# Expert layers over all tokens replaced by chosen experts on sorted rows, with result transfers placed between row transfers on GpSimd

## What is computed

```python
def reference(x, queries, ln1_w, ln2_w, wqkv, wo, gate_w, w13, w2):
    x = x + linear_attention(layernorm(x), queries)
    return x + ffn(layernorm(x), ...)
# ffn:
    h = rmsnorm(x, ln1_w); q, k, v = split(h @ wqkv.T); q, k = rope(q), rope(k)
    x = x + softmax(causal(q @ k.T * scale)) @ v @ wo.T
    h = rmsnorm(x, ln2_w).reshape(-1, HID)
    rprobs = softmax(h @ gate_w.T)
    topw, topi = top_k(rprobs, 2); topw = topw / sum(topw)
    wfull = zeros((T, E)).at[arange(T)[:, None], topi].set(topw)
    for e in range(8):
        w1, w3 = w13[e, :256], w13[e, 256:]
        out = out + ((silu(h @ w1.T) * (h @ w3.T)) @ w2[e].T) * wfull[:, e:e + 1]
    return x + out
```

## Time and profile before

| | us |
|---|---|
| median of 3 runs (lowest 431.62, highest 436.45) | 433.2 |
| the profiled execution: device time | 435.69 |
| its span in the profile | 434.0 |
| PE busy in the span | 415.7 (96%) |
| DVE busy | 342.6 (79%) |
| ACT busy | 287.8 (66%) |
| POOL busy | 216.6 (50%) |

### The profile page before, as it was taken

One profiled execution on the slowest core, in us unless ns is written; L12 is line 12 of the kernel. 1 busy time (PEld: TensorE's weight loads), 2 busy tenths in 40 slices (PEclk: granted clock), 3 DMA queues, 4 the chain that ended last, 5 costly groups with the idle time before them and its releaser, 6 DMA issues.

```text
span 434.0 us, 8892 instructions
## 1 busy us (share of the span) xinstructions
PE 415.7 (96%) x3032; PEld 255.0 (59%) x3032; DVE 342.6 (79%) x569; ACT 287.8 (66%) x577; POOL 216.6 (50%) x359
## 2 busy tenths in 40 slices
PE   8987997999999999999999999999999999999995
PEld 4743444545455454554545445468788877888883
DVE  6895688779889898998989976546668998787773
ACT  3743653778878688786877869765775565555552
POOL 5100646336147364473744034135883886676673
PEclk9998985599999999999999999899999999999999
DMA  7914202001611010100100000043221223421200
GB/s 219 319 47 137 57 2 56 2 2 40 201 34 28 4 59 0 34 26 4 57 3 5 0 3 3 2 76 74 62 58 37 87 60 66 97 66 57 95 1 24
DMA packets 16983, 23.92 MB, mean 55 GB/s; under 512 B 2622, under 2 KB 7614, under 8 KB 16942
## 3 DMA queue, kind: packets, MB, share of 16 engines
q1 hardware_dynamic: 15982, 22.21, 18.5%
q0 software_dynamic: 960, 1.18, 1.1%
HBM read 18.08 MB, written 5.05 MB: 53 GB/s over the span
## 4 chain that ended last, share of the span: by engine, by line
PE 67%; DVE 16%; issue 9%; ACT 4%; POOL 2%; DMA 1%; POOLq 0%; DVEq 0%; ACTq 0%
PE o_bank L1503 16%; PE tb L1486 11%; PE sp L1443 10%; PE tb L1635 6%; PE sp L1635 6%; DVE mx L1089 5%; PE o_bank L1611 4%; DVE mx L1087 3%; PE sp L1449 2%; PE sp L1463 2%; PE o_bank L1614 2%; ACT pt L893 2%; DVE sw L1287 2%; POOL gl L668 1%; DVE stats L984 1%
## 5 line engine op out<-in xcount | busy, mean ns | idle before, releaser
L893 ACT ACTIVATE pt<-tb 128x512 f32<-128x512 f32 (+2 forms) x310 | 153.4, 564 | 51.6 <-PE tb L1486 46.1
L1089 DVE TENSOR_REDUCE mx<-sp 128x2 f32<-128x1024 f32 (+1 forms) x128 | 143.4, 1155 | 22.5 <-PE sp L1449 13.6
L668 POOL TENSOR_TENSOR gl<-gg,gh 128x512 fp32r<-128x512 f32 x64 | 89.1, 1394 | 46.5 <-ACT gh L944 46.3
L1443 PE MATMUL sp<-k_stk,q_stk 62*128 62x512 f32 (+3 forms) x384 | 83.8, 432 | 4.1 <-DVE mx L1089 1.0
L1486 PE MATMUL tb<-q_stk,k_stk 64*128 64x512 f32 (+3 forms) x372 | 85.4, 413 | 1.6 <-ACT pt L893 1.1
L1503 PE MATMUL o_bank<-pt,v_all 128*32 128x512 f32 (+3 forms) x768 | 82.4, 511 | 0.0
L643 POOL TENSOR_TENSOR tick<-tick 128x1 f32<-128x1 f32 x96 | 18.8, 196 | 120.5 <-ACT pt L893 120.1
L1486 PEld LDWEIGHTS tb<-q_stk,k_stk 64*128 64x128 f32 x372 | 43.1, 193 | 51.0 <-ACT pt L893 40.9
L1287 DVE TENSOR_TENSOR sw<-silu,wbc 128x512 f32<-128x512 f32 x62 | 54.6, 881 | 21.1 <-ACT silu L955 20.8
L955 ACT ACTIVATE silu<-tb 128x512 f32<-128x512 f32 x64 | 38.2, 597 | 38.1 <-PE tb L1635 37.8
L1443 PEld LDWEIGHTS sp<-k_stk,q_stk 62*128 62x128 f32 x384 | 41.7, 198 | 28.1 <-DVE mx L1089 11.4
(11 more groups left out here) (224 smaller groups left out, 577.5 us busy)
## 6 DMA issues: line engine op xcount, KB each, us to landing
wbc<-g_scr SPq DMA_DIRECT2D x31, 256.0 KB, 3.3
w13r<-w_t SPq DMA_DIRECT2D x1, 2048.0 KB, 10.6
q_scr<-q_hi SPq DMA_DIRECT2D x8, 256.0 KB, 3.0
q_stk<-q_scr SPq DMA_DIRECT2D x20, 96.0 KB
x<-x_in SPq DMA_DIRECT2D x4, 256.0 KB, 3.8
q_scr<-q_lo SPq DMA_DIRECT2D x4, 256.0 KB, 3.3
result<-x SPq DMA_DIRECT2D x4, 256.0 KB, 2.5
k_stk<-k_scr SPq DMA_DIRECT2D x10, 96.0 KB
```

Of the source, the lines that this page charges most:

```text
L668: pool.tensor_tensor(gl[m % 4][:, :], gg[m % NGG][:, :], gh[m % 4][:, :].bitcast(F), ALU.subtract).then_inc(d_lo, 1)
L893: act.activation(pt[:, p0:p0 + 2 * len(heads) - 1:2, 0:w], src, ACT.Exp).then_inc(e_done, 1)
L1089: dve.reduce_max(half[:, :, t, i % TC], src[:, :, 0:w], AX.X).then_inc(s_free, 1)
L1443: last = pe.matmul(dst[:, k, w * x:w * (x + 1)], q_stk[n % NQ][rows_[k], i // TC, pair, P * (i % TC):P * (i % TC + 1)], k_stk[n % NQ][rows ...
```

## The change

Each token's row of 128 features is written twice, once for each of its two experts, into a DRAM tensor `xs_d` where the rows stand sorted by expert, each expert's part filled up to a multiple of 128 rows. That gives at most NT = 23 tiles of 128 rows a batch. A 129th column holds the row's place in the result. All multiplications of the third stage are now in plain fp32 (`w13`, `w2` are used as loaded), one tile at a time, with the expert's number in a register of PE; the gates are applied when the results are added to x.

- **Routing.** DVE works out each row's place (`places`, `c_rows`) and each tile's expert (`c_experts`); PE counts with `ranks`.
- **Sending.** POOL writes the rows with indirect DMAs (`send`), 16 of 128 rows a batch. SP fills `xs_d` with zeros ahead of it (`fill`, 12 transfers in periods 3 to 6) and reads the sorted rows back (`load_rows`, 5 transfers).
- **A tile j**: transpose (`turn_rows`), times ln2 on ACT, one matmul with 512 columns (`up`), silu on ACT, product on DVE, two transposes (`turn_products`), a copy on DVE, two matmuls of 128 columns (`down`), a copy on ACT; POOL writes the 128 rows to their places in `z_d` with an indirect DMA (`bring_back`), 23 a batch. At the end SP loads `z_d` (`load_results`) and DVE adds (`add_up`).
- **Batch 0's steps** move from period 7 into periods 4 (attn), 5 (wo, square, norm, htr) and 6 (logits, choice, places), as words of `EXTRA`, and its 16 sends stand between the masks of periods 6 and 7. The fp32r halves of weights and activations and their transfers are gone.
- **Batch 1's steps** stand between batch 0's tiles, as before between steps; its sends follow behind the 11th result of batch 0, one result brought back behind each.

```diff
+EXTRA = {
+    4: {"s7.0.0": "c.a0", "s5.2.1": "c.a1"},
+    5: {"s1.2.0": "c.w0", "s6.1.0": "c.w1", "p2": "x.sq0", "p3": "x.sq1", "p4.0": "x.sq2", "p4.1": "x.sq3",
...
+SENDS = 4
...
 SECOND = {
...
+    "pe": {-1: "o1", 0: "attn0 attn1", 2: "wo0 wo1", 7: "htr0 htr1", 9: "logits", 13: "rank"},
...
+    "dve": {-1: "o1", 2: "sum0", 3: "sum1", 5: "norm0", 6: "norm1", 9: "first", 10: "equal lead", 11: "rest second",
+            12: "sums", 13: "places", 15: "gates"},
 }
-ROOT = 8
...
+NT = (NPAIR + E * (P - 1)) // P
...
+LOADS = ((0, 2), (2, 5), (5, 11), (11, 17), (17, NT))
+OUTS_ROOT, OUTS_FIRST = 4, 11
+ADD_AT = 16, 19
...
+            def load_rows(b):
+                sp.wait_ge(sent[b], 16 * 2 * T)
+                for q, (j0, j1) in enumerate(LOADS):
+                    sp.dma_start(xs[b][:, j0:j1, :], xs_d[b][P * j0:P * j1, :].rearrange("(j p) w -> p j w", p=P)
+                                 ).then_inc(ld_rows[b][q], 16)
...
+            def load_results(b):
+                sp.wait_ge(back[b], 16 * NT)
...
+            def send(b, i):
+
+                k, t = i % 2, i // 2
+                pool.indirect_dma_start(xs_d[b], bass.IndirectOffsetOnAxis(ap=pos[b][:, k, t:t + 1], axis=0),
+                                        h2x[b][k][:, t, :], None, bounds_check=NT * P - 1,
+                                        oob_is_err=False).then_inc(sent[b], 16)
...
+                    elif s == TC and n == 6:
+                        twin()
+                        pool.wait_ge(ld_fill, 16 * B * N_FILL)
+                        pool.wait_ge(c_pos, 1)
+                        for _ in range(SENDS):
+                            send(0, next(sends))
...
+                        if n == NG - 1 or (n == NG - 2 and s >= TC):
+                            for i in itertools.islice(sends, 1):
+                                send(0, i)
...
+            add_residual(0)
+            for j in range(OUTS_FIRST):
+                bring_back(0, j)
+                if j + 1 == OUTS_ROOT:
+                    c_root(1)
+            pool.wait_ge(c_pos, 2)
+            pool.wait_ge(c_h, 4)
+            pool.wait_ge(c_tw, 4)
+            for i in range(2 * T):
+                send(1, i)
+                if OUTS_FIRST + i < NT:
+                    bring_back(0, OUTS_FIRST + i)
+            add_residual(1)
+            for j in range(NT):
+                bring_back(1, j)
...
+            def add_up(b, c):
+
+                dve.wait_ge(ld_z[b][c], 32)
+                dve.wait_ge(d_x, 2 * b + c + 1)
+                for k in range(2):
+                    for t in range(TC * c, TC * (c + 1)):
+                        row = x[:, T * b + t, :]
+                        last = dve.scalar_tensor_tensor(row, z[b][:, k, t, :], gate_w[:, b, k, t:t + 1], row,
+                                                        ALU.mult, ALU.add)
...
+            for b in range(B):
+                pe.wait_ge(c_te, b + 1)
...
+                for j in range(-2, NT + 2):
+                    if j + 2 < NT:
+                        turn_rows(b, j + 2)
+                    if 0 <= j < NT:
+                        up(NT * b + j, of[j])
+                    if j >= 2:
+                        down(NT * b + j - 2, of[j - 2])
+                    if 1 <= j <= NT:
+                        turn_products(NT * b + j - 1)
+                    if b == 0:
+                        second("pe", STEPS, j)
```

More of the change, by code:

```diff
@@ L842, in c_square @@
[L842 to L850 removed]
+                        k = T + i
+                        last = act.activation(h2x[1][1][:, i, 0:HID], y[:, k, :], ACT.Copy, scale=rms[:, k:k + 1])
@@ new lines, in take_out @@
+            def take_out(b, j):
+                i = NT * b + j
+                act.wait_ge(p_y, i + 1)
+                act.copy(y_out[b][:, j, :], YB[i % 2][:, 0:HID]).then_inc(e_y, 1)
+            for b in range(B):
+                for j in range(-2, NT + 2):
+                    if j + 2 < NT:
+                        turned(NT * b + j + 2)
+                    if 0 <= j < NT:
+                        gate(NT * b + j)
+                    if j >= 2:
+                        take_out(b, j - 2)
+                    if b == 0:
+                        second("act", STEPS, j)
@@ L1309, in _ @@
+            for b in range(B):
+                for j in range(-2, NT + 1):
+                    if 0 <= j < NT:
+                        product(NT * b + j)
+                    if j > 0:
+                        turned(NT * b + j - 1)
+                    if b == 0:
+                        second("dve", STEPS, j)
+                    elif j in ADD_AT:
+                        add_up(0, ADD_AT.index(j))
+            for c in range(NC_):
+                add_up(1, c)
         @block.tensor
@@ new lines, in ranks @@
+            def ranks(bank):
+                earlier = bank[:, 0:(T + 1) * E].rearrange("p (t e) -> p t e", e=E)
+                pe.matmul(earlier, before_bf[:, :], chosen[:, :, :], start=True, stop=False)
+                for t in range(T):
+                    last = pe.matmul(earlier[:, t + 1:T + 1, :], all_bf[:, :],
+                                     chosen[:, t:t + 1, :].broadcast_to([P, T - t, E]), start=False, stop=t == T - 1)
+                return last
+            def c_logits(b, X):
+                pe.wait_ge(c_cp, 2)
+                logits(1, X[0]).then_inc(c_lg, 1)
@@ new lines, in up, with turn_products @@
+            def up(i, e):
+                pe.wait_ge(e_xt, i + 1)
+                if i >= 2:
+                    pe.wait_ge(e_g, i - 1)
+                pe.matmul(AB[i % 2], xt[i % 3][:, :], w13[:, e, :], start=True, stop=True).then_inc(p_ab, 1)
+            def turn_products(i):
+                pe.wait_ge(e_g, i + 1)
+                if i:
+                    pe.wait_ge(e_gt, i)
+                for f in range(2):
+                    last = pe.transpose(GT[:, P * f:P * (f + 1)], gg[i % 2][:, P * f:P * (f + 1)], ident[:, :])
+                last.then_inc(p_gt, 1)
```

697 lines of the change are left out of this document (325 added, 372 removed), and 4 rows, old and new, of the table EXTRA.

## The result

| | before | after |
|---|---|---|
| median | 432.5 us (4 runs, 431.6 to 436.5) | 446.9 us (4 runs, 445.2 to 449.5) |
| ratio | | 1.029 (95%: 1.023 to 1.035) |
| profiled execution: device time, span | 435.7, 434.0 | 446.7, 445.0 |
| PE busy in the span | 415.7 | 373.9 |

PE has 42 us less to do, and the program takes 14 us longer. The time lies above the range of 416 to 443. Medians and lowest and highest times are over all executions; every ratio leaves out those that took over 1.5% longer than the fastest of their kernel.

The account below looks back on a forecast made before the run. PE was taken to set the pace almost everywhere. Expert stage from 289.2, batch 1's places 329.2, first `up` 366.1, its tiles to 414.3, then 14.45 gave a span of 428.8 and 428.0 us; range 416 to 443.

Parts of the forecast that it names:

- start of the expert stage: Softmax periods: 285.5 with +1.2, +3.4, +4.7 and −6.6 for periods 4 to 7 and +1.0 for masks gives 289.2.
- from there to batch 1's places: Batch 0's tiles: pipeline filling 2.5, then 37.5 for 14 tiles, batch 1's steps, clock and a wait; places at 329.2.
- 28 issues: POOL between the batches: 12 sends and 12 results in turn, then 4 sends, at 1.1 us each, 30.8 us.
- from the last issue to the first `up`: Batch 1's rows: landing 2.5, SP's load of two tiles 2.9, transpose and copy 0.7; first `up` at 366.1.
- 23 tiles to the last result: Batch 1: tiles 41.4, clock 3.0, batch 0's `add_up` 1.0, the last tile's way through the engines 2.8; to 414.3.
- the end: Behind the last tile: last result's issue 1.1, landing 2.5, loads and additions 8.05, store 2.8; 14.45 us.
- Both meet: Period 6: PE's work of 30.9 us and DVE's of 30.8 were taken to coincide, so the period grows by 4.7.
- The sends of batch 0: POOL, periods 6 and 7: 16 sends and 12 masks take 25 us for about as much time; 1.0 added.
- The second way to a dear transfer: DVE and POOL get into each other's way: DVE's product 881 ns beside POOL's work, 688 with one operand in PSUM.
- The order: Between the batches PE waits 19 us, 347 to 366, as 12 results stand ahead of or between needed rows.
- a dear transfer: Rival: indirect transfers on POOL cost 1.5 us each, the 28 issues 11.2 more, 442.6 in all; chance 0.22.
- The rival of bound handovers: Expert tiles: handovers between engines bind at 2.1 us a tile, 11.1 more, 439.1 in all; chance 0.15.

Follow-up runs that it names:

- the seven traces: Profiled executions of the changed kernel and six follow-up kernels with the same work in period 6 but for the sends; period 6 took 35.25 to 37.97 us.
- the kernel without the choice: Changed kernel, batch 0's 16 sends issued behind the last mask, most of DVE's choice and places of period 6 left out; 457.8 us, period 6 30.92 us.
- the sends first: Changed kernel with all 16 sends of batch 1 issued ahead of the 12 results that stood between them; 433.1 us, 0.995 of before.
- the kernel with the places earlier: Batch 1's sends ahead of the 12 results, its steps nearer together, and 8 results instead of 11 ahead of its sends; 428.4 us, ratio 0.983.

## Why the prediction was wrong, step by step

The span was forecast at 428.8 and is 445.0, 16.2 us more. Where they lie, forecast and measured:

| step | forecast | measured | difference |
|---|---|---|---|
| start of the expert stage | 289.2 | 302.7 | +13.5 |
| from there to batch 1's places | 40.0 | 42.2 | +2.2 |
| 28 issues | 30.8 | 35.4 | +4.6 |
| from the last issue to the first `up` | 6.1 | 6.0 | −0.1 |
| 23 tiles to the last result | 48.2 | 45.4 | −2.8 |
| the end | 14.45 | 13.2 | −1.2 |

**The softmax periods failed.** Period 4 came out at +2.4 (forecast +1.2), period 5 at +6.6 (+3.4), period 6 at +11.2 (+4.7), period 7 at −0.8 (−5.6 with the masks). Period 4 began 2.2 us earlier than before, which says nothing: in the seven traces that have the same instructions up to there it began between 175.4 and 180.2. The step that failed most is period 6: "PE gets logits 1.9, ranks about 1.0 and the clock's 1.4: 30.9. DVE gets 28 small operations ... 30.8. Both meet". DVE's 30.3 us of work came as forecast. PE's own work was even less, since the ranks took 0.4 (0.3 in the kernel without the choice) where I had 1.0:

```profile
238.86 1.95 PE L1636 MATMUL sp<-gate_sb,h2t 128*128 128x8 f32 x16
240.75 0.38 PE L1512 MATMUL sp<-k_stk,q_stk 62*128 62x256 f32 x2
...
254.50 0.22 PE L1643 MATMUL sp<-chosen,before_bf 128*128 128x72 bf16 x1 [0.99 <-DVE chosen L1272]
...
254.91 1.51 PE L1574 MATMUL o_bank<-pt,v_all 128*32 128x256 f32 x16
```

What was wrong are the clock and the waits, and "Both meet", which has no room for either. By PE's busy time the 38.0 us are, as an estimate: 26.6 as before, logits 1.9 and ranks 0.3 at full clock, 5.7 for running at the lower clock (34.50 busy less these 28.8) where I had 1.4, and 3.5 in which PE idled (37.97 − 34.50) where I had nothing; 3.3 of these were waits for DVE's row maxima and choice. Two engines with 29 and 30 us of work that wait for each other did not finish in 30.8, and PE's clock was lower with the choice in the period (0.77 to 0.90 in seven traces) than without it (0.94 in two). By the runs, the choice is 6.7 us of the period, the short matmuls 2.2, the sends none. The lesson of the earlier trace rows had been read for the gap between the batches only; period 6 has it too:

```profile
240.00:245.00 5.00, 5.00 (x42) 3.06 (x41) 2.37 (x3) 1.70 (x4) 1.01 (x4) 0.66 0.62 149
245.00:250.00 5.00, 3.99 (x44) 1.89 (x43) 4.76 (x12) 3.25 (x8) 2.65 (x9) 1.00 0.01 1
250.00:255.00 5.00, 3.66 (x33) 1.73 (x37) 4.86 (x9) 2.17 (x4) 0.98 (x1) 0.64 0.00 0
255.00:260.00 5.00, 4.83 (x40) 2.92 (x40) 3.83 (x13) 2.98 (x6) 0.00 (x0) 0.68 0.01 3
260.00:265.00 5.00, 4.06 (x28) 1.59 (x28) 4.64 (x9) 3.02 (x7) 3.81 (x4) 0.67 0.12 40
```

0.66 stands behind the logits, 0.64 to 0.68 where DVE was busy 3.8 to 4.9 of 5 us and PE waited for row maxima and for the choice; the stretch of 245 to 250, with DVE as busy and PE idle for a fifth, still had 1.00. What exactly takes the clock down inside the period stays open. Period 7 was forecast at 21.0, and 1.0 for the masks, and took 26.8. Without sends and choice it took 23.3 at full clock (23.7 with the last eight matmuls), so 2.7 of the miss are PE's and ACT's own pace, and some 2 the clock: the same instructions took 25.9 at 0.87. Periods 4 and 5 add 1.2 and 3.2 to the miss; a third of the latter is ACT's, the rest was not tested.

**The sends of batch 0 were judged about right**: +1.0 forecast, 1.0 measured in period 7 at the same clock, within the scatter of that period.

**The transfer was judged nearly right, and its miss is the second largest of the table, 4.6 us over the 28 issues.** 1.1 was forecast for one; it is 0.97 on the engine and 1.27 from start to start. The 0.30 between two were the part that I had not thought of: busy time alone would have passed as 1.0. The Trainium skill, "DMA: Bandwidth & Descriptors", section "Latency and other measured facts", with its 1 us for a GpSimd transfer's first byte, would have been near the busy time, but it is not what one transfer costs the next. The text's own point, "from 1.29 us on the gain is gone", met the measured 1.27 almost exactly: with the rest as forecast the kernel would have been even.

**The second way to a dear transfer did not show in this kernel.** A send took 0.97 us at 350, where DVE was busy about half of the time (2.37 of 5 us), and 0.97 at 370, where it was idle. The Trainium skill, "SBUF — State Buffer", section "SBUF: two separate sides", has such a conflict for descriptors; these rows show none, and none of DVE's operations beside them had both operands in SBUF.

**The order was judged right.** "Between 347 and 366 PE waits 19 us ... 12 results of batch 0 stand ahead of or between rows for which PE waits": the wait is 23.1 us, released by a load of `xs` as foretold, POOL never waits for a tile in these 28 issues, and taking the results out of the way gave 13.8 us. I forecast a net gain with this loss inside it, and the loss inside was as large as the whole difference.

**The tiles were judged slightly too dear**: 1.63 us from one to the next in the middle of batch 1 (392.56 to 417.05 for 15), 1.8 forecast, "with 1.65 and 2.1 as ends", so it lies just below the lower end. The rival of bound handovers fell. Two of ACT's copies of a result:

```profile
392.56 0.27 ACT L1015 COPY y_out<-o_bank 128x128 f32<-128x128 f32 x1
394.19 0.27 ACT L1015 COPY y_out<-tb 128x128 f32<-128x128 f32 x1
```

**The chances.** Slower had 0.28, all of it through a dear transfer or bound handovers; the transfer came at 1.27, not 1.5, and the handovers did not bind. No rival said that the softmax periods could cost 13.5 us more; their terms were single numbers without ends, and the range took nothing from them.

## What to carry to other kernels

On a queue that feeds a later stage, what somebody waits for goes first, and what nobody waits for fills the holes; each of 12 results ahead of a row cost its full 1.27 us. When small work is moved into a stretch where two engines already hand over to each other at nearly full load, the larger of their busy times is a lower bound (here 30.8 forecast, 38.0 measured): put ends on it, and count what PE's clock does when it starts to wait. An earlier result only helps if the next thing in line (here the 16 sends) is also early.

## What the hardware showed that I had not expected

- An indirect GpSimd transfer costs its instruction: 0.97 us for 128 rows, 0.91 for 64, 0.84 for 16, and 0.30 more before the next starts; beside the masks of period 7 a pair of mask and send took 1.7 to 2.0 us.
- The granted clock in period 5 differs from execution to execution of the same instructions: 1.00 in the changed kernel (33.44 us), 0.95 with the sends first (34.47), 0.86 in the kernel with the places earlier:

```profile
208.81:245.36 36.55, 34.91 (x294) 17.64 (x291) 26.66 (x34) 24.70 (x66) 12.37 (x31) 0.86 0.16 40
```

  3.1 us for the same work, which is why the kernels here are compared by stage, and perhaps part of why 10 runs of one kernel spread over 9 us.
- ACT's normalisations of 128 elements took 0.52 us each beside the exps in period 5, its squares 0.32 and 0.21 more for reading the sum.
